# A four-layer Perceiver stack on one core: first loads split and reordered, VectorE's opening steps and GpSimd's last-layer work placed elsewhere

## What is computed

```python
x0 = _layernorm(x)
for l in range(4):
    h = rmsnorm(x0, n1[l])
    q, k, v = split(h @ Wqkv[l].T + bqkv[l]); q, k = apply_rope(q), apply_rope(k)   # 16 heads of 16
    x0 = x0 + sdpa(q, k, v, causal) @ Wo[l].T + bo[l]
    x0 = x0 + cross_attention(rmsnorm(x0, n2[l]), ctx, band from token ids)
    h3 = rmsnorm(x0, n3[l])
    x0 = x0 + silu(h3 @ Wg[l].T) * (h3 @ Wu[l].T) @ Wd[l].T
x = x + rmsnorm(x0, nf)
x = x + layernorm(y + window_attention(y)) * gamma + beta      # y = _layernorm(x), 16 tokens back
x = x + bitlinear_ffn(_layernorm(x))                           # weights rounded to -1, 0, 1
```

## Time and profile before

| | |
|---|---|
| median of 3 runs | 576.91 us (576.56 to 578.18) |
| the profiled execution | 576.95 us, of which 575.2 us are the span |
| PE busy | 524.7 us (91%) |
| PEld busy | 408.0 us (71%) |
| DVE busy | 350.7 us (61%) |
| ACT busy | 283.2 us (49%) |
| POOL busy | 113.6 us (20%) |
| chain that ended last | PE 77%, DVE 12%, ACT 8%, issue 2%, POOL 1% |

### The profile page before, as it was taken

The page is one execution under the profiler, slowest core; times in us unless marked ns, Lnnn a source line. Parts: engine busy times, 40 slices in busy tenths (PEclk is TensorE's granted clock), DMA queues, the critical chain, the costliest instruction groups (busy, mean ns, idle before and its releaser), DMA issues.

```text
span 575.2 us, 15277 instructions
## 1 busy us (share of the span) xinstructions
PE 524.7 (91%) x6585; PEld 408.0 (71%) x6586; DVE 350.7 (61%) x669; ACT 283.2 (49%) x509; POOL 113.6 (20%) x126
## 2 busy tenths in 40 slices
PE   4988898999998999999998989999989989999766
PEld 2666665988777666988676659988767669987514
DVE  5878257567565555665654675573755556652896
ACT  1164754632445465433356547343475767426442
POOL 5241200012241100011514000020621001631100
PEclk9999999999999999999999999999999999999977
DMA  8300071020420010200501200203200200000001
GB/s 326 157 2 2 3 286 46 2 74 1 179 80 3 6 70 3 74 0 1 221 2 39 75 2 1 74 1 111 112 15 17 76 1 2 1 0 2 2 2 42
DMA packets 4683, 30.40 MB, mean 53 GB/s; under 512 B 1153, under 2 KB 1665, under 8 KB 2818
## 3 DMA queue, kind: packets, MB, share of 16 engines
q1 hardware_dynamic: 4610, 29.35, 13.7%
HBM read 28.82 MB, written 0.52 MB: 51 GB/s over the span
## 4 chain that ended last, share of the span: by engine, by line
PE 77%; DVE 12%; ACT 8%; issue 2%; POOL 1%; DVEq 0%; POOLq 0%
PE psD L349 16%; PE QD L691 14%; PE psD L704 10%; PE QD L445 8%; DVE AQ L1902 5%; PE QD L485 5%; ACT PTR L1337 4%; PE psD L343 3%; PE psD L505 3%; PE QD L478 3%; PE psD L691 2%; PE psD L526 2%; PE psD L512 2%; PE psD L386 2%; DVE MX L1899 2%
## 5 line engine op out<-in xcount | busy, mean ns | idle before, releaser
L1337 ACT ACTIVATE PTR<-QD 128x2048 f32<-128x2048 f32 x40 | 75.2, 1880 | 53.0 <-PE QD L485 46.2
L1902 DVE TENSOR_REDUCE AQ<-QD 128x8 f32<-128x2048 f32 (+1 forms) x24 | 55.0, 2292 | 30.0 <-PE QD L445 29.9
L691 PE MATMUL QD<-HH,WFH 128*128 128x256 f32 x224 | 69.0, 308 | 0.0
L2590 POOL TENSOR_TENSOR rstd<-ms,mhalf 128x2 f32<-128x2 f32 x26 | 18.2, 699 | 234.1 <-ACT HE L1303 231.4
L691 PE MATMUL QD<-HL,WFH 128*128 128x256 f32 x224 | 63.3, 282 | 0.0
L691 PE MATMUL QD<-HH,WFL 128*128 128x256 f32 x224 | 63.2, 282 | 0.0
L1899 DVE TENSOR_REDUCE MX<-QD 128x16 f32<-128x2048 f32 x16 | 36.7, 2293 | 39.6 <-PE QD L445 39.6
L704 PE MATMUL psD<-WC,HID 128*128 128x256 f32 x256 | 58.5, 381 | 0.0
L2007 DVE TENSOR_TENSOR WFL<-WC,WFH 128x512 fp32r<-128x512 f32 x64 | 44.8, 707 | 18.4 <-ACT WFH L1383 18.1
L349 PE MATMUL psD<-WAB,hT 128*128 128x256 f32 (+1 forms) x152 | 53.6, 490 | 0.8 <-DVE hT L1840 0.8
L2637 POOL TENSOR_SCALAR_AFFINE_SELECT PTR<-PTR 128x1024 f32<-128x1024 f32 (+1 forms) x24 | 34.5, 1440 | 93.1 <-ACT PTR L1337 93.1
(11 more groups left out here) (187 smaller groups left out, 976.9 us busy)
## 6 DMA issues: line engine op xcount, KB each, us to landing
WC<-in_wc SPq DMA_DIRECT2D x4, 3072.0 KB, 10.8
WAB<-in_wa SPq DMA_DIRECT2D x4, 1024.0 KB, 7.1
WAB<-in_wb SPq DMA_DIRECT2D x4, 1024.0 KB, 4.8
WF<-in_wf SPq DMA_DIRECT2D x1, 3072.0 KB, 11.1
bias<-in_bias SPq DMA_DIRECT2D x4, 512.0 KB, 5.5
WAB<-in_wt SPq DMA_DIRECT2D x1, 1024.0 KB, 5.5
X<-in_x SPq DMA_DIRECT2D x2, 256.0 KB, 2.8
out_x<-XE SPq DMA_DIRECT2D x4, 128.0 KB, 2.3
```

Of the source, the lines that this page charges most:

```text
L691: mm = pe.matmul(S[:, w * L:(w + 1) * L], wp[:, m, :], hp[:, k, :], start=(k == 0 and j == 0), stop=(k == KT - 1 and j == 2))
L1337: nc.scalar.activation(PTR[:, r % 2, :], QD[:, :], ACT.Exp, scale=SCALE if r < SELF_ROUNDS else 1.0).then_inc(t_exp, 1)
L1902: v = dve.tensor_reduce(QKR[b][:, t, 0, h, MAXROW].rearrange("p (s r) -> p r s", r=SG_H), QD[:, :].rearrange("p (r s n) -> p r s n", r=4, ...
```

## The change

The first loads are cut into pieces, each with a semaphore of its own, and issued in another order: input of batch 0, identity alone (64 KB), `nrm`, the query and key columns of Wqkv (512 KB), input of batch 1, bias of queries and keys (256 KB), the rest of `const` (292 KB), the value columns (256 KB), the other half of the bias (256 KB), Wo (256 KB), and then as before. Fifteen transfers take the place of eleven. TensorE starts on the identity alone and expands the causal mask after `queries_keys`. VectorE starts before the pads are set, casts the constants later, and keeps the residual stream of batch 0 after `weigh_T(0, 0, 1)`. GpSimd waits for `const` later, and adds the output bias of batch 0 after two `sines`. In the last layer `value_pads` has one more wait and stands before `weigh_last(0)`; `scale_ternary(1)` and `(2)` stand together after `add_beta(0)`.

```diff
 # tensor
-                pe.wait_ge(wa_ld, l * 16 + 16)
+                pe.wait_ge(*((wa_ld, l * 16 + 16) if l else (wqk_ld, 16)))      # queries_keys; values: wv_ld
...
+                if l == 0 and use == "wo0":
+                    pe.wait_ge(wa_ld, 16)
...
-            pe.wait_ge(c_ld, 16)
+            pe.wait_ge(id_ld, 16)
             norm_T(0, 0, 0)
-            causal_strips()
             queries_keys(0, 0, 0)
             queries_keys(0, 0, 1)
+            causal_strips()
             norm_T(0, 0, 1)
             values(0, 0)
 # sync
+            first_input(0)
+            sp.dma_start(ident, const_in[:, C_ID:C_ID + P]).then_inc(id_ld, 16)
             sp.dma_start(nrm[:, :], nrm_in[0]).then_inc(nrm_ld, 16)
+            first_qkv(0, 2 * D).then_inc(wqk_ld, 16)
+            first_input(1)
+            first_bias(0, 2 * D).then_inc(bqk_ld, 16)
+            sp.dma_start(const[:, C_CAUSAL:], const_in[:, C_CAUSAL:]).then_inc(c_ld, 16)
+            first_qkv(2 * D, 3 * D).then_inc(wv_ld, 16)
+            first_bias(2 * D, 4 * D).then_inc(bias_ld, 16)
+            sp.dma_start(Wo, wa_in[0][:, WA_O:WA_N].rearrange("p (k n) -> p k n", k=KT)).then_inc(wa_ld, 16)
 # vector
             def small_constants():
+                dve.wait_ge(id_ld, 16)
+                dve.tensor_copy(identB[:, :], ident)
                 dve.wait_ge(c_ld, 16)
-                dve.tensor_copy(identB[:, :], ident)
...
-            dve.wait_ge(pads_set, 1)
             layernorm_stats(0, 0, X0)
             centre(0)
-            small_constants()
             first_mean_square(0)
             weigh_T(0, 0, 0)
+            dve.wait_ge(pads_set, 1)
             layernorm_stats(1, 1, X0)
             first_mean_square(1)
             first_scale(0)
+            small_constants()
             centre(1)
-            layernorm_apply(0, 0, X0, X, lambda v: v.then_inc(x_kept[0], 1))
             biased_qk(0, 0, 0)
             cosines(0, 0, 0)
             key_sines(0, 0)
             biased_qk(0, 0, 1)
             add_sines(0, 0, 0)
             weigh_T(0, 0, 1)
+            layernorm_apply(0, 0, X0, X, lambda v: v.then_inc(x_kept[0], 1))
             biased_v(0, 0)
             key_sines(0, 1)
 # gpsimd
             def value_pads():
                 pool.wait_ge(*filled(NL - 1, "cwo1"))
+                pool.wait_ge(hx_set, NL * B)
...
-            pool.wait_ge(c_ld, 16)
             rsqrt(0, 0, 0)
             ln_rsqrt(0)
             ln_rsqrt(1)
-            add_bo(0, 0)
             rsqrt(0, 0, 1)
+            pool.wait_ge(c_ld, 16)
             sines(0, 0, 0)
             sines(0, 0, 1)
+            add_bo(0, 0)
...
                 rsqrt(NL - 1, 2, 1)
+                value_pads()
                 weigh_last(0)
-                scale_ternary(1)
-                value_pads()
                 rsqrt(NL, 0, 0)
-                scale_ternary(2)
                 ln_rsqrt(2)
                 add_beta(0)
+                scale_ternary(1)
+                scale_ternary(2)
                 weigh_last(1)
```

More of the change, by code:

```diff
@@ L211, in perceiver @@
         c_ld, seg_ld, vec_ld = sem("c_ld"), sem("seg_ld"), sem("vec_ld")
+        id_ld, wqk_ld, wv_ld, bqk_ld = sem("id_ld"), sem("wqk_ld"), sem("wv_ld"), sem("bqk_ld")
         x_ld = [sem(f"x_ld{b}") for b in range(B)]
@@ L370, in values @@
                 pe.wait_ge(*emptied(l, f"n0{b}"))
-                pe.wait_ge(wa_ld, l * 16 + 16)
+                pe.wait_ge(*((wa_ld, l * 16 + 16) if l else (wv_ld, 16)))
                 use = f"v{b}"
@@ L1239, in _, with first_input, first_qkv, first_bias @@
         def _(sp):
-            for b in range(B):
+            def first_input(b):
                 sp.dma_start(X0[:, 2 * b:2 * b + 2, :], x_in[:, 2 * b:2 * b + 2, :]).then_inc(x_ld[b], 16)
-            sp.dma_start(const[:, :], const_in).then_inc(c_ld, 16)
-            sp.dma_start(nrm[:, :], nrm_in[0]).then_inc(nrm_ld, 16)
-            sp.dma_start(WA, wa_in[0]).then_inc(wa_ld, 16)
-            sp.dma_start(bias[:, :], bias_in[0:1, :].broadcast_to([P, 4 * D])).then_inc(bias_ld, 16)
+            def first_qkv(n0, n1):
+                return sp.dma_start(Wqkv[:, :, n0:n1], wa_in[0][:, WA_QKV:WA_O].rearrange("p (k n) -> p k n", k=KT)[:, :, n0:n1])
+            def first_bias(n0, n1):
+                return sp.dma_start(bias[:, n0:n1], bias_in[0:1, n0:n1].broadcast_to([P, n1 - n0]))
+            first_input(0)
+            sp.dma_start(ident, const_in[:, C_ID:C_ID + P]).then_inc(id_ld, 16)
+            sp.dma_start(nrm[:, :], nrm_in[0]).then_inc(nrm_ld, 16)
+            first_qkv(0, 2 * D).then_inc(wqk_ld, 16)
[5 more added lines that the diff above has]
+            sp.dma_start(Wo, wa_in[0][:, WA_O:WA_N].rearrange("p (k n) -> p k n", k=KT)).then_inc(wa_ld, 16)
             sp.dma_start(rowI[:, :], seg_in[4 * P:8 * P].rearrange("(a n) -> a n", a=1)).then_inc(seg_ld, 16)
@@ L1845, in biased_qk @@
                 use = f"qk{b}{t}"
-                dve.wait_ge(bias_ld, l * 16 + 16)
+                dve.wait_ge(*((bias_ld, l * 16 + 16) if l else (bqk_ld, 16)))
                 dve.wait_ge(rstd_set[b], l * NORMS + 1)
```

## The result

The changed kernel took 574.72 us in the median of 7 runs (574.39 to 576.38), the kernel before, run in turn with it, 577.38 us (575.80 to 578.63). The ratio is 0.9958, 95% interval 0.9939 to 0.9977: 2.66 us less. The profiled execution took 574.83 us with a span of 573.1. The forecast of 576.2 and its range (575.3 to 577.5) lie above the result.

A forecast was written before the change was run, and what follows sets the result against it. TensorE, busy 91% of the span, was taken as the bound, so other engines count only where it waits. From 576.95 us, 0.76 off for the opening and 0 for the last layer gave 576.2, range 575.3 to 577.5.

The forecast's parts named there:

- the 5.1 of my line: Opening: query and key columns, ending 835 KB into the queue, land at 5.1 us, by a line between two earlier landings.
- rival C: Opening: query and key columns land late; landing at 8.85 us gives 577.5 us; chance 0.12.
- 0.24 more for each instruction that overlaps: Opening, VectorE's `key_sines` beside GpSimd's `add_bo`: one or both of the pair hit, 0.36 us taken, bounds 0 and 0.48.
- the last layer at nothing: Last layer: VectorE gets 1.7 us back, but TensorE doesn't wait, so worth 0; bounds 0.6 us lost, 0.5 gained.
- D: Last layer: VectorE's 1.7 + 0.59 us reach the end, 573.9 us; chance 0.07.
- E: Last layer: scalings beside VectorE's window work make batch 1 late, 0.8 us lost, 577.0 us; chance 0.04.
- What TensorE makes of 1.35 us: Opening: how much of TensorE's 1.35 us earlier start survives, depending on when its half pace doubles.
- A: Opening: the doubling moves with the work, queries and keys full at 13.59, gain 0.76, 576.2 us; chance 0.45.
- B: Opening: the doubling stays at 13.65 us, queries and keys full at 14.26, gain 0.26, 576.7 us; chance 0.27.
- slow in any case: Opening: the first half's four query and key records run at half pace, full at 11.47 in place of 12.82.
- Sum: Whole kernel: 576.95 - 0.76 for the opening + 0 for the last layer = 576.2 us.
- no correction: Base of the forecast: the profiled execution, 0.04 above the median of three runs, was taken as it stood, 576.95.

The follow-up runs named there:

- only the tail held: Kernel before, and changed kernel, with 42 unread extra TensorE products between 541 and 566 us: 575.76 us (0.9980) and 575.49 us (0.9976).
- the weights cut: Kernel before with only the first load of Wqkv and Wo cut into three pieces: 577.67 us, ratio 1.0002.
- before, opening held: Kernel before with 11, 2 and 4 unread extra TensorE products in the opening, none in the tail: 574.90 us, ratio 0.9971.
- the changed kernel with the opening held: Changed kernel with 9 unread extra TensorE products ahead of the first transposes and 2 behind: 573.84 us (0.9932), later 574.11 us (0.9963).
- both held: Unread extra TensorE products in opening and tail: kernel before 574.49 us (0.9953), changed kernel 574.45 us (0.9957).
- 11 and 2 products: Kernel before with eleven unread extra TensorE products from 1.3 us on and two behind the first transposes: 574.70 us, ratio 0.9955.

## Why the prediction was wrong, point by point

**Right: the start.** The statistics began at 3.38 (3.65 forecast), the queries and keys at 7.38 (7.60). The weights landed at 2.18 + 4.4 = 6.6, later than the 5.1 of my line, but in time; rival C falls. The constants landed at 3.64 + 5.3 = 8.9, and VectorE's first cast that reads them started at 9.42. (The 1907 KB of the line are 1895 by the sizes in the trace, which moves its result by 0.01 us.)

**Right in size, one term by luck: VectorE and GpSimd.** The moved mask cost 0.34 us (12.54 to 12.88; 0.3 forecast). The `key_sines` pair took 0.91 us instead of 0.48 beside `add_bo`, 0.43 more (0.36 taken, 0.48 the bound). But it was not "0.24 more for each instruction that overlaps". One of the pair was hit, the other was not:

```profile
16.81 0.70 DVE L1894 TENSOR_TENSOR HID<-HID,const 128x128 f32<-128x128 f32 x1
17.44 0.28 DVE L1894 TENSOR_TENSOR HID<-HID,const 128x128 f32<-128x128 f32 x1
```

The first ended at 17.51, 0.15 us after `add_bo` (16.19 + 1.18 = 17.37). In the kernel before the pair's 0.52 us each had hidden the same thing, because GpSimd's two `sines` ended one behind the other:

```profile
13.67 0.94 POOL L2617 TENSOR_TENSOR HID<-HID,const 128x128 f32<-128x128 f32 x1
14.24 0.52 DVE L1878 TENSOR_TENSOR HID<-HID,const 128x128 f32<-128x128 f32 x1
```

Here too VectorE's ended 0.15 us after GpSimd's (14.76 against 14.61), and the second of the pair 0.15 us after the second `sines` (14.68 + 0.52 against 14.57 + 0.48). So what such an overlap costs is set, in these rows, by how much of GpSimd's instruction is left: the bound of 0.48 had no ground, and that 0.43 came near the 0.36 is due to where the two happened to fall. VectorE became the bound before the first maxima: `add_sines` starts at 18.38 and is 0.67 long, against scores ready at 17.29 + 1.17 = 18.46. What the sum left out is next: TensorE's transposes now wait for it, and of the 1.40 us won at the first maxima 0.13 are lost at the second.

**Right: the last layer at nothing.** 1.7 us of VectorE's time came back and no wait of TensorE went with them. Rivals D and E fall, by the chain and by the run of that part alone.

**Wrong: "What TensorE makes of 1.35 us".** A had the doubling move by 1.35 us, B had it stay. It came between 10.10 and 10.73, where A gives 12.3 and the kernel before had 13.65; the queries and keys ended 2.33 us earlier and the first maxima came 1.40 us earlier, where the sum had 0.76. The first half was to be "slow in any case" and full at 11.47: it was full at 7.38 + 3.53 = 10.91, and as VectorE bounds the rest, its taking them at 11.04 and not at 11.49 is what counted. Measured over kernels that share an opening, the doubling varies: between 12.2 and 13.0 us with only the tail held, 13.65 in the profiled execution of before, at about 14.3 with the weights cut, later than 15.1 with the new last layer alone. In the five changed openings that aren't held it lies between 10.1 and 11.9. The Trainium skill, "TensorE: Matmul & The Clock Gate", section "What's actually happening", says that the release follows activity and falls differently from run to run against the same work; the traces agree. In the prediction it stood beside the choice between A and B, but a spread of the doubling around either was not put into the range.

**Wrong: "Sum".** It was made against one execution with "no correction". The medians of before were later 576.80 to 577.66 on four chips and 577.38 beside the changed kernel. From 577.38 the same sum gives 576.62, farther from 574.72: the low base made the forecast look better by 0.43 us, by luck. The gain was sized at 0.76 and is 2.66. Of the 1.90 between, 0.51 lie before the second maxima (1.27 less 0.76), 1.02 behind them, 0.54 between profiles and medians, less the 0.17 given back.

**Wrong: no term for the tail.** "From where score and maximum follow each other" the sum took every later step as unchanged. But in the last 30 us, in which VectorE sets the pace, the granted clock fell to 0.50 at some time in every trace without extra products there. Of the 2.29 us between the last outputs 1.02 arose behind the second maxima: the kernels are 1.24 us apart at the transpositions of the last layer, 0.95 at 561 us, 2.29 at the end. Holding the clock there alone took 1.1 us from the kernel before and nothing measurable from the changed one.

**What the 2.66 us are, then.** With the extra products in both places the two kernels agree within 0.1 us (574.49 and 574.45). Held in the opening alone they differ by 0.79 in the medians and by 0.10 at the second maxima of the traces; in the traces of the pair held in both places it is 0.76. So by the medians the new opening by itself is worth something between 0 and 0.8 us, which these runs don't settle. The rest of the gain, two thirds or more of it by the medians, goes when the extra products stand in both kernels: that is TensorE's pace, in an opening whose work begins earlier and of which more runs at 2.4 GHz, and in a tail that loses less. That the early start is what brings it is argued from the undone wait for the pads and from the table, with one trace for each kernel. A rival is the landing of the first weights, which moved the start of the old opening between 8.68 and 10.17. It is not the gain: cutting that load alone gave none (577.67), nor with the extra products in both places (574.35 against 574.49).

**Left open.** Why the tail of the changed kernel loses less. Half pace up to 570 us stands in five of six traces with a tail that isn't held and an opening of before or with the pads awaited, and in none of the six with the changed opening. But the one with full pace from the first product on (before, opening held) is free of it, and the times of the changed kernel with the opening held fall in two groups as well (eight at 573.16 to 574.71, four at 575.63 to 576.11), as if it came there too, only less often. Nor need an upper group be the tail: with both places held, two and three runs of the kernels with the changed opening still stand above 575.3, against one in 24 with that of before, and the one trace of these has its fall at 17 us. Whether the shift of some 2 us against the clock's falls decides this, or chance in so few traces, no run here tells.

## What to carry to other kernels

Where TensorE's first products run at half pace, an edit that lets TensorE begin earlier can be worth more than the time by which it begins earlier, and its worth can't be sized from one execution: compare where the weight loads' distance halves in several. Look for the same thing at the end of the kernel, wherever another engine sets the pace. Before an order of loads is tuned, hold the clock with products that nobody reads: here 17 in the opening gave the kernel before 2.0 us, where the whole change gave 2.66, and with 42 more in the tail it gained 3.2 and its scatter went from 5.2 to 0.8 us, with no other step moved. And where two engines' instructions slow each other, look at single instructions and at when each ends, not at the mean of a pair.

## What the runs showed of the hardware

- The granted clock stands at 1.00 from 7 to 20 us in executions whose weight loads are 0.85 us apart (before, changed) and in others whose loads are 0.43 apart (both held). The pace before the first doubling shows only in the loads; a later fall shows in the granted clock too (0.50 from 10.4 to 13.7 us with 11 and 2 products, loads 0.85 apart).
- A fall of TensorE's clock in the tail, among small products between waits, cost something or nothing by when it came: with 0.50 from 558 to 564.75 us the tail was 546.12 us long, as long as with 1.00 throughout (546.12 to 546.33), with 0.50 up to 570 it was 547.39 or more.
- The same transfer of 1024 KB, issued at 2.65 us in the same place of the queue, landed after 5.9 us in one execution, 6.2 in two, and 7.2 to 7.4 in three.
- A product of 128 x 128 on VectorE with both inputs in on-chip memory, 0.28 us alone, took 0.52 beside a like product of GpSimd and 0.70 beside its addition of 128 x 512 (1.18 us), and each time ended 0.15 us after GpSimd's instruction. The fills of GpSimd that ran all the while beside VectorE's first statistics in the changed kernel (3.38 to 4.13) lengthened nothing: 0.75 us as before.
